# A cross-attention kernel whose first head is computed in two passes, each with its own running maximum

## The reference

```python
q = (x @ Wq).reshape(B, S, HEADS, DIM_HEAD).transpose(0, 2, 1, 3)
k = (context @ Wk).reshape(B, L, HEADS, DIM_HEAD).transpose(0, 2, 1, 3)
v = (context @ Wv).reshape(B, L, HEADS, DIM_HEAD).transpose(0, 2, 1, 3)
attn = jax.nn.softmax(jnp.einsum('bhsd,bhld->bhsl', q, k) * scale, axis=-1)
out = jnp.einsum('bhsl,bhld->bhsd', attn, v)
return out.transpose(0, 2, 1, 3).reshape(B, S, INNER) @ Wo + bo
```

## Time and profile before

| | |
|---|---|
| median of 3 runs | 1462.62 us (1462.29 to 1463.74) |
| profiled execution | 1464.52 us, its span 1462.7 us |
| PE, DVE, ACT, POOL busy | 95, 75, 54, 64% |
| mean granted clock of TensorE | 0.954 of full speed |
| head 0's maxima stage | 294.6 to 359.1 us |
| head 0's blocks 0 to 12, key projection to key projection | 369.36 to 486.31 us |

### The profile page before, as it was taken

The page is one execution under the profiler, slowest core; times in us unless marked ns, Lnnn a source line. Parts: engine busy times, 40 slices in busy tenths (PEclk is TensorE's granted clock), DMA queues, the critical chain, the costliest instruction groups (busy, mean ns, idle before and its releaser), DMA issues.

```text
span 1462.7 us, 19933 instructions
## 1 busy us (share of the span) xinstructions
PE 1391.6 (95%) x6191; PEld 793.8 (54%) x6191; DVE 1095.5 (75%) x1484; ACT 793.9 (54%) x1576; POOL 941.2 (64%) x542
## 2 busy tenths in 40 slices
PE   5999998887999999999999999999999999998898
PEld 3877775533455555555554555455555555554565
DVE  8976666388888788778868878887887886666555
ACT  3458886321556556556655655555555555553332
POOL 5001113231889888978988897898898899886110
PEclk8999999655999999999999999999999999998799
DMA  6630000310000200100020020002002000000011
GB/s 173 206 126 18 18 17 7 71 22 2 0 1 1 49 1 1 33 17 1 1 49 1 1 46 4 1 1 49 1 0 47 1 1 1 1 1 13 18 38 40
DMA packets 77372, 39.45 MB, mean 27 GB/s; under 512 B 62047, under 2 KB 70000, under 8 KB 77002
## 3 DMA queue, kind: packets, MB, share of 16 engines
q1 hardware_dynamic: 77290, 38.36, 10.5%
HBM read 24.66 MB, written 13.68 MB: 26 GB/s over the span
## 4 chain that ended last, share of the span: by engine, by line
PE 86%; DVE 8%; DMA 3%; ACT 2%; issue 1%; POOL 0%; SPq 0%; ACTq 0%; DVEq 0%; POOLq 0%
PE ps L1384 24%; PE ps L1371 14%; PE ps L1372 12%; PE ps L1337 9%; DVE chunk_max L943 3%; DMA v_scratch<-v_stage 3%; PE ps L1324 3%; PE ps L1528 2%; PE ps L1199 2%; PE ps L1197 2%; PE ps L1208 2%; PE ps L1198 2%; PE ps L1209 2%; PE ps L1210 2%; PE ps L1316 1%
## 5 line engine op out<-in xcount | busy, mean ns | idle before, releaser
L524 POOL TENSOR_TENSOR psums<-psums,probs 126x1024 f32<-126x1024 f32 (+1 forms) x392 | 821.2, 2095 | 122.6 <-ACT probs L705 75.7
L705 ACT ACTIVATE probs<-ps 126x512 f32<-126x512 f32 (+1 forms) x816 | 416.2, 619 | 273.2 <-PE ps L1372 272.3
L943 DVE TENSOR_REDUCE chunk_max<-ps 128x2 f32<-128x1008 f32 (+1 forms) x416 | 472.7, 1181 | 77.1 <-PE ps L1337 75.7
L1384 PE MATMUL ps<-probs,v_mem 126*64 126x512 f32 (+1 forms) x1632 | 389.7, 598 | 0.0
L1371 PE MATMUL ps<-q_heads,ring 128*126 128x512 f32 (+1 forms) x816 | 342.9, 420 | 1.1
L1372 PE MATMUL ps<-q_low,ring 128*126 128x512 f32 (+1 forms) x816 | 322.5, 395 | 0.0
L994 DVE TENSOR_TENSOR xn<-xn,probs 126x512 f32<-126x512 f32 x126 | 231.1, 1834 | 29.9 <-ACT probs L705 25.6
L671 ACT CAST ring<-ps 64x252 fp32r<-64x252 f32 (+1 forms) x356 | 128.1, 360 | 136.3 <-PE ps L1324 133.2
L1384 PEld LDWEIGHTS ps<-probs,v_mem 126*64 126x64 f32 (+1 forms) x1632 | 111.5, 136 | 165.5 <-issue 120.9
L1371 PEld LDWEIGHTS ps<-q_heads,ring 128*126 128x126 f32 (+1 forms) x816 | 152.0, 186 | 88.6 <-issue 44.5
L1337 PE MATMUL ps<-ring,q_heads 64*128 64x504 f32 (+1 forms) x416 | 171.9, 482 | 18.1 <-DVE chunk_max L943 9.7
(11 more groups left out here) (200 smaller groups left out, 1412.8 us busy)
## 6 DMA issues: line engine op xcount, KB each, us to landing
v_scratch<-v_stage SPq DMA_DIRECT2D x51, 252.0 KB
v_mem<-v_scratch SPq DMA_DIRECT2D x8, 1606.5 KB
ctx_mem<-in_ctx_t SPq DMA_DIRECT2D x3, 803.2 KB, 8.9
vslot<-in_ctx_rows SPq DMA_DIRECT2D x51, 47.2 KB
pair_w<-in_f_pairs SPq DMA_DIRECT2D x17, 128.0 KB, 2.1
pair_w<-in_f_pairs SPq DMA_DIRECT2D x17, 65.0 KB, 1.8
x_tok<-in_x SPq DMA_DIRECT2D x1, 512.0 KB, 4.1
wo<-in_c_wo SPq DMA_DIRECT2D x1, 512.0 KB
```

The source lines that it names most:

```text
L524: pool.tensor_tensor(sums[0:r, 0:width], sums[0:r, 0:width], probs[0:r, n % PROBS, 0:width], ALU.add).then_inc(c_sum, 1)
L705: act.activation(probs[0:r, n % PROBS, cols(half)], ps[0:r, score_bank(t, half), :], ACT.Exp, scale=float(HD) ** -0.5).then_inc(c_exped, 1)
L943: dve.tensor_reduce(chunk_max[:, h % 2, i:i + 2, c], ps[:, banks[0]:banks[1] + 1, 0:group_tiles(c) * KT], AX, ALU.max).then_inc(c_reduced, 1)
L1384: ins = pe.matmul(ps[half * HD:(half + 1) * HD, B_ACC, :], v_tiles[0:r, h % 2, t, :], probs[0:r, n % PROBS, cols(half)], start=(t == 0), s ...
```

## The change

Head 0 becomes two passes. Pass 0 takes tiles 0 to 23 with the maximum of the first 6 groups, pass 1 tiles 24 to 50 with the maximum of groups 6 to 12. Each pass has its own shift, accumulation and sums; at the end the two are joined by shares, exp(maximum of the pass less maximum of both), divided by the joint sum. The stage ahead runs 24 steps in place of 52, with a key projection after every second step. The other 28 run in head 0's blocks: 7 steps each in blocks 0 to 3, 5, 9, 10 and 11, 6 in blocks 4, 6, 7 and 8, 4 in block 12. Two of them, *late*, stand after the second tile's values, on banks (3,4) and (0,1). In head 0 DVE adds no rows and POOL adds all tiles full width. New in head 0: `row_shift(1)` and `shift(1)` in block 4, `first_shares` after it, `sum_rows(0)` in block 8, a copy of the accumulator in block 6; the query projection moves from blocks 5, 6 to 6, 7. In head 1 pass 0's output projection stands in blocks 2 and 3 and pass 1's in 8 and 9. `pass_of(h, t)` is h + 1 but 0 for tiles below 24 of head 0, and semaphore counts are renumbered to match.

```diff
+LATE_PAIRS = ((3, 4), (0, 1))
...
+SPLIT = 6
+SPLIT_T = SPLIT * GT
...
+def pass_of(h, t):
+    return h + 1 if h or t >= SPLIT_T else 0
...
+    if h == 0 and b < GROUPS_H - 1:
+        small = [c for c in range(b) if first_head_small(c)]
+        at = SPLIT * STEPS + 7 * b - len(small)
+        middle = 0 if first_head_small(b) else 1
+        steps = list(range(at, at + 6 + middle))
+        return steps[:2], steps[2:2 + middle], steps[2 + middle:4 + middle], steps[4 + middle:]
     group = GROUPS_H * h + b + AHEAD - 1
     if group >= GROUPS_H * HEADS:
-        return [], [], []
+        return [], [], [], []
     steps = [group * STEPS + i for i in range(STEPS)]
-    middle = [GROUPS_H * STEPS + b] if h == 0 and b < STEPS else []
-    return steps[:2], middle, steps[2:]
+    return steps[:2], [], steps[2:], []
...
+def first_head_small(b):
+    return b in (4, 6, 7, 8)
...
-    return h == HEADS - 1 or t % GT == GT - 1
+    return h == HEADS - 1 or h and t % GT == GT - 1
...
+                    p = pass_of(h, t)
+                    first = first_tile(p)
+                    if t == first:
+                        continue
+                    sums = psums[:, h % 2, :] if p else psums_0
...
-                if g in (EARLY[2] + 1, EARLY[2] + 2):
-                    q_hi(1, g - EARLY[2] - 1, B_AUX)
-            q_rows(1)
+                if g in (EARLY[2] + 2, EARLY[2] + 4):
+                    q_hi(1, (g - EARLY[2]) // 2 - 1, B_AUX)
...
+                    if b == SPLIT and h == 0:
+                        acc_out(0)
...
+                    if h == 0 and b in (0, 1):
+                        q_rows(b + 1)
+                    if h == 0 and b == 5:
+                        act.wait_ge(c_mix, 2)
+                        act.activation(first_share[:, :, :], first_share[:, :, :], ACT.Exp,
+                                       scale=float(HD) ** -0.5).then_inc(c_mix, 1)
+                    if b == queries_in(h) + 2 and h + 2 < HEADS:
...
+            def first_shares():
+                dve.wait_ge(c_found, 2)
+                dve.tensor_tensor(first_sums[:, 0, :], f32(first_max[:, 0, :]), f32(first_max[:, 1, :]), ALU.max).then_inc(c_mix, 1)
+                dve.wait_ge(c_mix, 1)
+                dve.tensor_tensor(first_share[:, :, :], f32(first_max[:, :, :]),
+                                  first_sums[:, 0, :].unsqueeze(1).to_broadcast([P, 2, TT]), ALU.subtract).then_inc(c_mix, 1)
...
+                elif p == 0:
+                    dve.wait_ge(c_mix, 3)
+                    dve.tensor_tensor(first_sums[:, 1, :], sums, first_share[:, 0, :], ALU.mult).then_inc(c_rden, 1)
+                else:
+                    dve.wait_ge(c_rden, 1)
+                    dve.tensor_tensor(first_sums[:, 0, :], sums, first_share[:, 1, :], ALU.mult).then_inc(c_mix, 1)
+                    dve.wait_ge(c_mix, 4)
+                    dve.tensor_tensor(first_sums[:, 0, :], first_sums[:, 0, :], first_sums[:, 1, :], ALU.add).then_inc(c_mix, 1)
+                    dve.wait_ge(c_mix, 5)
+                    dve.reciprocal(first_sums[:, 0, :], first_sums[:, 0, :]).then_inc(c_mix, 1)
+                    dve.wait_ge(c_mix, 6)
+                    dve.tensor_tensor(first_share[:, :, :], first_share[:, :, :],
+                                      first_sums[:, 0, :].unsqueeze(1).to_broadcast([P, 2, TT]), ALU.mult).then_inc(c_rden, 1)
...
-            for step in range(GROUPS_H * STEPS):
-                maxima(step, step, FIRST_PAIRS[step % 3])
+            for step in range(SPLIT * STEPS):
+                maxima(step, FIRST_PAIRS[step % 3])
...
+                    before, middle, behind, late = steps_in(h, b)
                     for k, step in enumerate(before):
-                        maxima(step, count + k, PAIRS[k])
+                        maxima(step, PAIRS[k])
                     if h == HEADS - 1:
                         for t in block_tiles(b)[:2]:
                             if t:
                                 add_rows(h, t)
+                    for step in middle:
+                        maxima(step, PAIRS[1])
                     if b == 1 and h:
-                        reciprocals(h - 1)
-                    if b in (2, 3) and h:
-                        add_output(h - 1, b - 2, PAIRS[1])
-                    if b in (5, 6) and h + 2 < HEADS:
-                        q_lo(h + 2, b - 5, B_AUX)
+                        reciprocals(h)
+                    if b == 8 and h == 0:
+                        reciprocals(0)
+                    for p in (0, 1) if h == 1 else (h,):
+                        part = b - output_in(p)
+                        if part in (0, 1) and h:
+                            add_output(p, part, PAIRS[1])
+                    part = b - queries_in(h)
+                    if part in (0, 1) and h + 2 < HEADS:
+                        q_lo(h + 2, part, B_AUX)
                     if b == GROUPS_H - 1 and h + 1 < HEADS:
-                        shift(h + 1)
-                    count += len(before)
-                    for step in middle:
-                        maxima(step, count, PAIRS[1])
-                        count += 1
-                    if h < HEADS - 1 and b:
+                        shift(h + 2)
+                    if b == 4 and h == 0:
+                        shift(1)
+                    if 0 < h < HEADS - 1 and b:
                         add_rows(h, b * GT - 1)
                     for k, step in enumerate(behind):
-                        maxima(step, count + k, PAIRS[k])
-                    count += len(behind)
-                    if b == GROUPS_H - 2 and h + 1 < HEADS:
-                        row_maxima(h + 1, count)
+                        maxima(step, PAIRS[k])
                     g = projected_in(h, b)
                     if g is not None:
                         k_lo(g, B_KEYS)
+                    for k, step in enumerate(late):
+                        maxima(step, LATE_PAIRS[k])
+                    if b == GROUPS_H - 2 and h + 1 < HEADS:
+                        row_maxima(h + 2)
+                    if b == 3 and h == 0:
+                        row_maxima(1)
+                    if b == 4 and h == 0:
+                        first_shares()
...
+                if k == 0 and late_before:
+                    pe.wait_ge(c_reduced, late_before)
...
-            for step in range(GROUPS_H * STEPS):
+            for step in range(SPLIT * STEPS):
...
-                if step % STEPS == 1 and early < AHEAD:
+                if step % 2 and early < AHEAD:
...
+            last_on = [SPLIT * STEPS, SPLIT * STEPS, 0]
+            pending = (c_shift, 2)
+            def free_pair(k):
+                pe.wait_ge(c_reduced, last_on[k])
+                if k and pending:
+                    pe.wait_ge(*pending)
...
+                    before, middle, behind, late = steps_in(h, b)
                     for k, step in enumerate(before):
-                        pe.wait_ge(c_reduced, count + k - 1)
-                        if k and h == 0 and b == 0:
-                            pe.wait_ge(c_shift, 2)
+                        free_pair(k)
+                        if k:
+                            pending = None
                         max_scores(step, PAIRS[k])
-                    reduced = count + len(before)
-                    count = reduced
+                        last_on[k] = step + 1
                     for t in block_tiles(b):
                         for half in range(2):
-                            scores1(h, t, half, reduced - len(before) // 2)
+                            scores1(h, t, half, last_on[0], last_on[2])
                         if t % GT == 2:
-                            if before:
-                                pe.wait_ge(c_reduced, reduced)
+                            free_pair(1)
                             for step in middle:
+                                pending = None
                                 max_scores(step, PAIRS[1])
-                                count += 1
+                                last_on[1] = step + 1
                             if b == 1 and h:
-                                sum_rows(h - 1)
-                            if b in (2, 3) and h:
-                                if b == 3:
-                                    pe.wait_ge(c_x, 2 * h - 1)
-                                project_out(h - 1, b - 2, PAIRS[1])
-                            if b in (5, 6) and h + 2 < HEADS:
-                                q_proj(h + 2, b - 5, B_AUX)
+                                sum_rows(h)
+                                pending = (c_rden, h + 1)
+                            if b == 8 and h == 0:
+                                sum_rows(0)
+                                pending = (c_rden, 1)
+                            for p in (0, 1) if h == 1 else (h,):
+                                part = b - output_in(p)
+                                if part in (0, 1) and h:
```

(33 more changed lines are left out.)

193 lines of the change are left out of this document (110 added, 83 removed).

## The result

The changed kernel takes 1471.68 us in the median of 4 runs (1468.99 to 1474.14), the kernel before beside it 1463.18 (1462.29 to 1464.93). The ratio is 1.0056, with a 95% interval from 1.0035 to 1.0077: about 8 us slower. The forecast was no change, 1462.4, in a range up to 1469. The profiled execution of after took 1468.99 us, its span 1467.1, against 1464.52 and 1462.7.

The account below looks back on a forecast made before the run. It took DVE to bound the stage of head 0's maxima and PE the blocks from block 0 on. Stage -28.8 and blocks and passes +28.6 gave -0.2 us, so 1462.4 us from the median 1462.62, range 1454 to 1469.

Parts of the forecast that it names:

- The late pair: Head 0's blocks 0 to 11: first score 5.55 us after the key projection, before 3.77; 1.78 us per block, +21.4 us.
- the second shift: Head 0's block 4: behind steps start 1.28 us apart instead of 0.34, plus two small matmuls of 0.5: +1.45 us.
- The middle step: Head 0's blocks: a middle step costs 0.68 us each, in eight blocks in place of four: +2.7 us.
- the sum over rows: Head 0's block 8: pass 0's sum over rows makes the block 11.07 us against 9.24: +1.8 us.
- the output projection in head 1: Head 1: the output projection of one pass more costs +2.1 us.
- Rival 1: Head 0's blocks: late pair hides, PE pays only 0.77 us per block, 1450.4 us; chance 0.30 whole or in part.
- The chained operations: End of pass 1: four small DVE operations replace one reciprocal; bounded by none and 1 us, taken as none.
- The stage: Head 0's maxima ahead of block 0: 52 steps become 24, clock up from 307; 28.8 us saved.
- rival 2: Stage ahead of head 0: clock stays low, key projections pace it, only 23.2 us saved, 1468.0 us; chance 0.22.
- other new waits: Unspecified new waits making the kernel slower, sharing chance 0.08 with the rival that POOL's additions carry head 0.

Follow-up runs that it names:

- late_first: The changed kernel, but DVE takes the first late maximum before the low parts of the new keys instead of behind them: 1471.09 us, ratio 1.0051.
- after_again: The changed kernel, unaltered, run and profiled again: 1470.57 us, ratio 1.0062.
- early_release: The changed kernel, but PE's second behind step in head 1's block 1 waits only for the first of DVE's four chained operations: 1466.98 us, ratio 1.0033.
- chain_dense: The changed kernel with the chain's intermediate in PSUM and the stage's odd steps and all from 16 on multiplied twice: 1463.99 us, ratio 0.9996.

## Why the prediction was wrong

**The late pair** was right: 5.52 us to the first score for 5.55, and 23.7 us from projection to projection over head 0 for 26.5. The other 2.8 are small things: the second shift, +1.45 foreseen, cost little in block 4, whose interval is 11.08 us where I had 12.5; and steps on a head's last group of three tiles have shorter maxima, 0.90 us each in block 4 (1.80 for two), where I had taken 1.16 for all. By `steps_in`, block 11 holds such steps of head 1's last group, and the intervals of blocks 11 and 12 are 0.4 to 0.5 us under my figures. The middle step (11.63 for the 11.70 of such a block), the sum over rows (12.74 for 12.8) and the output projection in head 1 (2.3 for 2.1) came as foreseen. Rival 1 is dead: the first score comes at 5.52 us and not at 4.6, DVE's maxima release PE in the block shown, and `late_first`, which takes ACT's copies out of the way, moved the first score by 0.09 us only.

**The chained operations** were the first of two steps that failed. I wrote "I bound them by none and 1 us, and take none, since PE issues a step and a score pair before it asks". The cover that I named was there: PE had other work until 499.77. But the chain ended 3.2 us behind that, at 502.97, and the block lasted 4.7 us longer: the stall, and behind it a slower clock, which cost 0.6 more in blocks 2 and 3. That is 5.2 us for a term that I had bounded by 1. I took the price from a reciprocal that reads PSUM and asked only how wide the operations are, not where their operands lie and what POOL does meanwhile. The PSUM chain gives 4.7 us back in the medians, and POOL kept short brings the two operations to 0.17 and 0.18 us: this cause is shown.

**The stage** was 2.9 us short in the profile. I had the clock up "from 307, as in the rows", since PE would be at least as dense. It was denser, and the clock rose 23 us in (after, `after_again`, `early_release`), or was down from its 6th us on at the latest (the other four of the seven below). From the first step to the projection, seven profiles of the changed kernel with this part as it was or with edits elsewhere show 48.18 to 51.93 us, in the middle 49.97: a typical saving of 24.8 us, not 26.5 as in the profile of after. That is rival 2 in nearly its full form. The pace at either clock was right: 3.34 us between projections foreseen and 3.31 measured at the low clock, 2.4 and 2.38 at the high one. At the low clock throughout 23.2 saved was foreseen, and 74.8 - 51.9 = 22.8 measured; the terms that I gave for it add up to 41.75 us and not to the 41.3 that I wrote, so they give 22.8 themselves. With the clock up from before the stage to its 24th us, which I had not priced, it saves 74.8 - 41.1 = 33.7. What the clock would do was the second step that failed, and what I hadn't seen is that the change swaps a stage that keeps its pace at either clock for one that depends on it.

**The sum by its parts:** stage -26.5 in the profile with its way into block 0 (foreseen -28.8), head 0 +23.7 (+26.5), chain +5.2 (0), output projection +2.3 (+2.1) is +4.7, and with -2.2 ahead of the stage and +1.9 behind head 1's block 11 the +4.4 of the two spans. Those last two I don't put down to the change: among the seven profiles the stage begins between 290.8 and 294.8 us, and the part behind head 1's block 11 takes 859.4 to 864.1 us, though no edit touches either. Against the medians' +8.5 some 1.7 more are the typical stage; the other 2 to 3 us are of the size of this spread, and I can't place them, since only a profiled run shows where its time went.

**The chances.** 0.30 for slower held both causes only half: rival 2 had 0.22, and a wait like the chain's was among "other new waits" at 0.08. Each alone gives a time inside the range (rival 2 1468.0, the chain 1467.6), the two together 1473.

Left open: why the clock doesn't rise for 20 us in a stage in which PE is busy without a gap by the profile, and why it falls at about 315 in the kernel with unread matmuls. The runs show that what PE does ahead of the stage matters, and that a clock which is up when the stage begins isn't enough; of denser matmuls in it they show no gain that is clear of noise.

The Trainium skill's rule that spoke against the high clock here (TensorE: Matmul & The Clock Gate, section A second HAM failure mode: psum-queue depth-cycling) pointed to the right side, the low clock. But it puts it down to short idles between matmul groups, and here the clock stayed at 0.50 with these filled, PE busy 8.00 us of 8 (`chain_dense`, 300 to 308).

## What to carry to other kernels

Price a small DVE operation by where its operands lie: if both are in SBUF and POOL is in a long operation beside it, count up to one whole POOL operation for each, and keep an intermediate in PSUM if PE waits for it. When a change takes work away from the engine that bounds a stage, ask how fast the next one is at the lower clock, and price it so unless a trace shows the clock up throughout it. A few unread matmuls in the gaps ahead of such a stage can be worth more than what the change was to bring: here some 11 us, by the two ratios 1.0018 with the PSUM chain alone and 0.9943 with them too. To see whether a stage goes by the clock, compare its pace at both levels, counted from the stage's own start.

## What the runs showed that I had not expected

An addition of DVE on 8 columns took 1.94 us beside POOL's additions and 0.17 without them, or with one operand in PSUM (0.17); a multiplication on 16 columns 2.22 against 0.18 and 0.17. Both ended 0.03 us behind the addition of POOL that was running. A stage in which the modelled PE was busy for all of 16 us ran at 1.2 GHz nearly throughout (300 to 316 with doubled steps), and one that was busy for 13.5 of 16 (296 to 312 with the unread matmuls ahead of it) at 2.4 GHz: the granted clock did not go with the busy share inside the stage. It did not go with its own level at the stage's first step either, since four profiles began high and lost it. And the clock's state there is worth 51.9 - 41.1 = 10.8 us of a stage of 24 steps, while the maxima of the same stage with 52 kept 1.13 us each at both levels.
